# An audio tower on one core: the attention stage's chunk buffer, ScalarE's order in a step, and what is issued at the change of batch

## The reference, cut to what matters

```python
h = tokens(x)                                       # 8 batches x 376 tokens x 256
h = h + attn(layernorm(h))                          # 16 heads of 64: q,k,v; rope; causal softmax; @ Wo + bo
h = h + moe(layernorm(h))                           # top 2 of 4 experts: router, gates, w1, w3, w2
# attention, for each head:
sim = where(causal, q @ k.T * scale, -inf); attn = softmax(sim); out = attn @ v
# layernorm: (x - mean) / sqrt(var + 1e-5)
```

## Time and profile before

| what | us |
|---|---|
| median of 3 runs (lowest to highest) | 1735.87 (1735.42 to 1737.89) |
| the profiled execution, its own time | 1737.82 |
| its span, first to last instruction | 1736.0 |
| TensorE busy in the span | 1465.3 |
| ScalarE, VectorE, GpSimd busy | 958.4, 1183.6, 845.4 |

### The profile page before, as it was taken

The page is one execution under the profiler, slowest core; times in us unless marked ns, Lnnn a source line. Parts: engine busy times, 40 slices in busy tenths (PEclk is TensorE's granted clock), DMA queues, the critical chain, the costliest instruction groups (busy, mean ns, idle before and its releaser), DMA issues. The chain is left out here.

```text
span 1736.0 us, 30153 instructions
## 1 busy us (share of the span) xinstructions
PE 1465.3 (84%) x10725; PEld 1371.8 (79%) x10725; DVE 1183.6 (68%) x2590; ACT 958.4 (55%) x2093; POOL 845.4 (49%) x705
## 2 busy tenths in 40 slices
PE   5389999999989998998399999999998756789039
PEld 4279888888889897988399999999998746788039
DVE  7548676767677777775245666666577389459896
ACT  5547575757576757674244444445443344459552
POOL 4468575868576767762345555545544433000000
PEclk8679999999999999998599999999999868899569
DMA  7490202021111111010467666566565421003313
GB/s 244 145 316 19 73 19 80 31 80 32 59 34 56 52 58 52 4 35 4 154 223 210 182 202 206 180 188 211 177 196 149 89 86 38 10 2 133 118 46 112
DMA packets 91309, 186.94 MB, mean 108 GB/s; under 512 B 8568, under 2 KB 64184, under 8 KB 90904
## 3 DMA queue, kind: packets, MB, share of 16 engines
q1 hardware_dynamic: 80648, 171.19, 29.0%
q0 software_dynamic: 10512, 13.83, 4.7%
HBM read 139.01 MB, written 59.35 MB: 114 GB/s over the span
## 5 line engine op out<-in xcount | busy, mean ns | idle before, releaser
L1647 POOL TENSOR_TENSOR expert_w<-expert_raw,expert_w 128x768 fp32r<-128x768 f32 x95 | 181.9, 1915 | 241.9 <-ACT expert_w L1471 241.9
L1429 PE MATMUL psum<-slots_high,expert_w 128*128 128x384 f32 x1216 | 289.9, 339 | 6.4 <-DVE expert_act L1613 5.1
L879 ACT ACTIVATE expert_raw<-psum,neg_max 120x376 f32<-120x376 f32 (+2 forms) x384 | 176.8, 486 | 106.0 <-DVE neg_max L1083 103.8
L1429 PEld LDWEIGHTS psum<-slots_high,expert_w 128*128 128x128 f32 x1216 | 211.6, 190 | 10.0 <-issue 8.3
L1509 ACT ACTIVATE expert_act_high<-expert_act 128x384 fp32r<-128x384 f32 x152 | 79.8, 525 | 181.0 <-DVE expert_act L1613 181.0
L1106 DVE TENSOR_TENSOR pt_low<-psum,pt_high 128x752 fp32r<-128x752 f32 x128 | 120.5, 942 | 81.2 <-ACT pt_high L888 80.8
L1440 PE MATMUL psum<-expert_w,expert_act_high 128*128 128x256 f32 x912 | 173.2, 286 | 3.1 <-ACT slot_out L1491 3.0
L1002 POOL TENSOR_TENSOR qk_low<-rotated,qk_high 128x376 fp32r<-128x376 f32 x128 | 127.0, 992 | 95.9 <-ACT qk_high L872 95.9
L1618 DVE TENSOR_TENSOR expert_act_low<-expert_act,expert_act_high 128x384 fp32r<-128x384 f32 x152 | 109.8, 722 | 79.7 <-ACT expert_act_high L1509 79.7
L1429 PE MATMUL psum<-slots_low,expert_w 128*128 128x384 f32 x608 | 155.7, 337 | 0.0
L1440 PEld LDWEIGHTS psum<-expert_w,expert_act_high 128*128 128x128 f32 x912 | 145.4, 189 | 5.6 <-ACT slot_out L1491 3.9
(11 more groups left out here) (303 smaller groups left out, 3982.6 us busy)
## 6 DMA issues: line engine op xcount, KB each, us to landing
expert_w<-experts_split SPq DMA_DIRECT2D x57, 768.0 KB, 4.3
expert_raw<-in_experts SPq DMA_DIRECT2D x107, 384.0 KB, 5.2
x_slots<-in_c_slots SPq DMA_DIRECT2D x4, 3168.0 KB, 27.6
slot_rows<-x_slots SPq DMA_DIRECT2D x19, 396.0 KB, 5.3
up_spill<-held SPq DMA_DIRECT2D x5, 1128.0 KB, 5.0
held<-up_spill SPq DMA_DIRECT2D x5, 1128.0 KB, 6.1
experts_split<-pt_high SPq DMA_DIRECT2D x12, 384.0 KB, 2.4
experts_split<-pt_low SPq DMA_DIRECT2D x12, 384.0 KB, 3.2
```

The lines of the kernel that those rows point to most:

```text
L879: last = act.activation(probs[0:ni, h % 2, at:at + P * it + ni], score_bank(h % 2, it), ACT.Exp, bias=neg_max[0:ni, h % 2, it:it + 1], acc ...
L1429: last = pe.matmul(psum[:, 2 * k + g % 2, 0:TILE_SLOTS], w[hw][:, f, at:at + P], xt[hx][:, i % 2, c, :], start=(n == c == 0), stop=(n == 2 ...
L1647: pool.tensor_tensor(w[1][:, g % RING, :], raw[:, r % RAW, :], w[0][:, g % RING, :].bitcast(F32), ALU.subtract).then_inc(w_low, 1)
```

## The change

- `whole` gets a tile of its own. The load of the first chunk of the coming change is issued a batch earlier, behind the last store of this one (for the first: behind SP's work of batch 0), and waits for POOL's `parts_low` only, not for the rotations.
- To make room, `mask_f`, `ident_f` and `before_f` (read only in the stage before) lie in `shared`'s columns of the probabilities, and the four small tables of `tile_table` in `resid`.
- `begin(b)` on ACT: `deviation(b-1)` is issued ahead of the value copies of the second tile, behind the splits. A one-column exponential into `exp_warm` is issued ahead of those of the third tile.
- `step` on ACT: `spread_inverses(b, c)` and `scale_rows(b-1, (c,))` are issued behind `raw_copy` of step `c`, ahead of the first exponential, in place of the end of the step (the first `spread_inverses` leaves the prologue). The wait for `parts_low` goes from step 0; that for `parts_stored` stays.
- `step` on DVE: `swap_pairs(ahead + 1)` is issued ahead of `inverses(c + 1)`.

```diff
@@ attention
-        whole = shared[:, 0:CHUNK_COLS]
+        whole = sb("whole_w", [P, CHUNK_COLS])
+        warm = sb("exp_warm", [P, 1])
@@ block.sync
                 def load_whole(j):
                     e, k = SPLIT_JOBS[j]
+                    if j:
+                        sp.wait_ge(parts_low, j)
-                    sp.dma_start(whole, a["experts"][e, KEPT_SPLIT[k], :, :]).then_inc(whole_in, 16)
+                    sp.dma_start(whole[:], a["experts"][e, KEPT_SPLIT[k], :, :]).then_inc(whole_in, 16)
...
                 for b in range(BATCH + 1):
+                    if b == 1:
+                        load_whole(0)
                     if b in SPLIT_BATCHES:
-                        sp.wait_ge(rot_made, 16 * b + 2 * LEAD + CR_ROT)
-                        load_whole(2 * b - 2)
                         store_parts(2 * b - 2)
                         load_whole(2 * b - 1)
                         store_parts(2 * b - 1)
+                        if 2 * b < len(SPLIT_JOBS):
+                            load_whole(2 * b)
@@ block.scalar begin(b)
                         if at == 1 and b in SPLIT_BATCHES:
                             split_part(2 * b - 2)
                             split_part(2 * b - 1)
+                        if b and at == 1:
+                            deviation(b - 1)
+                        if b and at == 2:
+                            act.activation(warm[:], consts[:, EPS_LN:EPS_LN + 1], ACT.Exp)
                         for half in range(2):
...
-                        if b and at == 1:
-                            deviation(b - 1)
@@ block.scalar step(b, c, more)
                     if c == 0 and b in SPLIT_BATCHES:
-                        act.wait_ge(parts_low, 2 * b)
                         act.wait_ge(parts_stored, 64 * b)
                     turned_high(b, 2 * c)
                     if c:
                         out_high(b, c - 1)
                     if projects:
                         raw_copy(b, ahead)
+                    spread_inverses(b, c)
+                    if b and c < T:
+                        scale_rows(b - 1, (c,))
...
-                    if more or c + 1 < PAIRS:
-                        spread_inverses(b, c + 1)
-                    if b and c < T:
-                        scale_rows(b - 1, (c,))
@@ block.vector step(b, c, more)
+                    if projects:
+                        swap_pairs(b, ahead + 1)
                     if more or c + 1 < PAIRS:
                         inverses(b, c + 1)
-                    if projects:
-                        swap_pairs(b, ahead + 1)
                     scale_out(b, c)
```

More of the change, by code:

```diff
@@ L69 @@
 STEPS_TO_NORM = 17
-TABLES = ("x_parts", "rope_sin", "attn_bo", "x_rows", "mask", "ident_b", "mask_f", "ident_f", "router_w", "router_bias",
-          "moe_consts", "row_ids", "before_f", "before", "ones_b", "slot_base")
+TABLES = ("x_parts", "rope_sin", "attn_bo", "x_rows", "mask", "ident_b", "router_w", "router_bias",
+          "moe_consts", "row_ids", "before", "ones_b", "slot_base")
 def attention_tables(nc, ctx):
@@ L81, in attention_tables @@
         sb("x_rows", [P, 2, TILES, ROW]), sb("mask", [P, 2, P], BF16), sb("ident_b", [P, 2, P], BF16),
-        sb("mask_f", [P, 2, P]), sb("ident_f", [P, 2, P]), sb("router_w", [P, 2, EXPERTS]),
+        sb("router_w", [P, 2, EXPERTS]),
         sb("router_bias", [P, EXPERTS]), sb("moe_consts", [P, MOE_COLS]), sb("row_ids", [P, ALL_TILES]),
-        sb("before_f", [P, P]), sb("before", [P, P], BF16), sb("ones_b", [P, P], BF16), sb("slot_base", [P, EXPERTS]))}
+        sb("before", [P, P], BF16), sb("ones_b", [P, P], BF16), sb("slot_base", [P, EXPERTS]))}
 def tokens_in(nc, psum, a, consts, ident, vec, decay, first, weights, h0_rows, x_dram, tables, cos, made):
@@ L445, in attention @@
         T = TILES
-        x, sin, bo, rows, mask, ident_b, _, _, w, bias, cm, ids, _, before, ones_b, base = (tables[n] for n in TABLES)
+        x, sin, bo, rows, mask, ident_b, w, bias, cm, ids, before, ones_b, base = (tables[n] for n in TABLES)
         wq, wk, wv = ([w.rearrange("p (c n) -> p c n", c=2) for w in weights[n]] for n in range(3))
@@ L490, in attention @@
         ends = sb("tile_ends", [P, EXPERTS])
[L491 to L494, removed]
+        past = resid[:, 0, 0:EXPERT_TILES * EXPERTS].rearrange("p (t e) -> p t e", e=EXPERTS)
+        place = resid[:, 1, 0:2 * EXPERT_TILES].rearrange("p (k t) -> p k t", k=2)
+        owner = resid[:, 1, 2 * EXPERT_TILES:3 * EXPERT_TILES]
+        start_of = resid[:, 1, 3 * EXPERT_TILES:4 * EXPERT_TILES]
         slots_cleared = sem("slots_cleared")
@@ L927, in split_part @@
                     act.wait_ge(parts_stored, 32 * j)
-                    act.activation(parts[0], whole, ACT.Copy).then_inc(parts_high, 1)
+                    act.activation(parts[0], whole[:], ACT.Copy).then_inc(parts_high, 1)
                 def begin(b):
@@ L981, in _ @@
                 exps(0, 1, TILE_ORDER)
-                spread_inverses(0, 0)
                 qk_split(0, 2 * LEAD - 2)
@@ L1006, in split_part @@
                     pool.wait_ge(parts_high, j + 1)
-                    pool.tensor_tensor(parts[1], whole, parts[0].bitcast(F32), ALU.subtract).then_inc(parts_low, 1)
+                    pool.tensor_tensor(parts[1], whole[:], parts[0].bitcast(F32), ALU.subtract).then_inc(parts_low, 1)
                 def scatter(b, pieces):
@@ L2368, in audio_tower @@
             tables = attention_tables(nc, attn)
+            mask_f, ident_f, before_f = (shared[:, 5 * TOK + at:5 * TOK + at + n] for at, n in ((0, 2 * P), (2 * P, 2 * P), (4 * P, P)))
+            tables |= {"mask_f": mask_f.rearrange("p (k n) -> p k n", k=2), "before_f": before_f,
+                       "ident_f": ident_f.rearrange("p (k n) -> p k n", k=2)}
             tokens_in(nc, psum, a, consts, ident, vec, decay, first, weights, h0_rows, x_dram, tables,
```

## The result

The changed kernel takes 1692.07 us, the median of 4 runs (1690.77 to 1693.29), against 1736.48 (1735.42 to 1737.89, 4 runs) for the kernel before on the same chip. The ratio is 0.9744, with a 95% interval from 0.9727 to 0.9761: faster by 44 us. The forecast was 1699. The profiled execution took 1693.09, its span is 1691.3, so the two profiled executions differ by 44.7 us.

A forecast was written before the change was run, and what follows sets the result against it. A ring through DVE and ACT was taken to pace attention steps, with chunk stores and a table load delaying step 0. 23.9 + 15.2 + 1.7 + 1.5 = 42.3, less about 4, left 38: 1699 us, range 1691 to 1706.

The forecast's parts named there:

- The mechanism: In attention, a loop of waits through DVE and ACT paces steps; chunk loads, stores and a table load delay step 0.
- The seven steps 0: First step behind each change of batch: 8.15 us each, together 80.94 down to 57.05, gaining 23.9 us.
- steps 1 to 6: Attention steps of batches 1 to 6: 50.85 against 53.39 us per batch, gaining 15.2 us in all.
- One sign: In step 0 behind a change, `pt_high` would be released by TensorE, not by a DMA; starting 1.6 us earlier.
- 4 us off for ties: Four chains in the new order within 0.1 us: 0.07 us off for each of 60 steps, leaving 38 of 42.3.
- the ring: Attention steps: DVE and ACT waiting on each other in a loop, 8.77 us, shrinking to 7.87, below TensorE's 8.1.
- GpSimd as the next bound of the scatter steps: In attention steps with a scatter, POOL's 7.82 us busy and 0.37 of small gaps would limit at about 8.2.
- changes alone: Rival: only the changes of batch gain, steps stay at 8.3 or more; gain 24 to 28, 1709 to 1712; chance 0.2.
- The margin of step 0: Behind a change, the second chunk's stores would land about 0.9 us before TensorE ends the turn that `pt_high` needs.
- steps alone pay: Rival: second chunk's load and stores keep `pt_high` late at six changes, copies late too; gain 26, 1711; chance 0.1.
- Swap blocks the reciprocal: Rival: DVE's swap waits for the second projection, costing 1.1 us in each of 61 steps; 1779 us; chance 0.04.
- It doesn't do what it says: Rival: table reload stays ahead of the first exponential, ACT's new work fills its gap; within 3 of 1736; chance 0.05.

The follow-up runs named there:

- the runs with the orders apart: From the changed kernel, VectorE's step order put back: 1704.46 us; in another run, ScalarE's step order put back instead: 1707.62 us.
- the first two experiments: The changed kernel with both step reorderings put back, 1713.68 us; the kernel before with only those two reorderings made, 1714.55 us.

## Why the prediction was right, and where its sizes were off

**The mechanism held in each step.** The rows that show it are the unhindered split at 355.38, `deviation`'s table load at 364.39, the second at 367.20 ahead of the one-column exponential, and the exponential at 373.27 with none; in the step, the swap ahead of the reciprocal. The seven steps 0 gained 23.5 (predicted 23.9), steps 1 to 6 15.6 (15.2), batch 7 1.8 (1.7), batch 0 1.3 (1.5), step 7 -0.9 (0): 41.3 where 42.3 were summed. The warm exponential and the deviation cost nothing at the copies, as said; with either of them elsewhere each change lost about 1 us. One sign failed in part: `pt_high` of step 0 was to be released by TensorE, and in the changes to batches 1, 2 and 6 it was still released by the stores.

**The term that was mis-sized: 4 us off for ties.** It rested on no row. Plain steps came at 8.17 in place of 8.1 (0.07, which is the tie's size), but those with a scatter came at 8.15 to 8.18 in place of 8.25, so the two errors cancel and the discount had nothing to stand for: the steps gained 18.7 of the 18.4 summed.

**A stretch taken at 0 that gave 3.2 us, though not through the change's parts.** From the last first projection to the expert matmuls the kernel before took 81.3 us, the changed one 78.1, but the kernel with the buffer and early load alone, in which these steps are as before, took 77.8 (768.52 to 846.30). All eleven other kernels took 77.2 to 79.6 here, whatever their parts; it is the profiled execution of the kernel before that is long. Windows 12 to 18 us behind the last first projection, before and then after:

```profile
793.70:799.70 6.00, 5.17 (x26) 5.02 (x26) 4.43 (x11) 4.28 (x16) 0.59 (x2) 0.63 0.01 3
```

```profile
752.04:758.04 6.00, 4.78 (x48) 4.48 (x47) 4.77 (x12) 4.30 (x16) 1.53 (x2) 1.00 0.01 3
```

The granted clock (third number from the end) was down to a mean of 0.63 of full there, and 1.00 after: 26 matmuls against 48 in six microseconds. What decides it in this thin end of the stage, where all kernels dip at some place, is open. So of 44.7 us some 41 are the change's parts, against 42.3 summed and 38 forecast; the 3.2 are luck as far as is known.

**A claim that was wrong without harm.** "With the ring out of the way a plain step can't go below about 8.1 us" read TensorE's busy 8.13 as its content. The content is 7.87 to 7.88, shown by step 0 of batch 3 and by the plain steps with the first maximum moved; the rest of the 8.13 went without any work being taken out. GpSimd as the next bound of the scatter steps at 8.2 was wrong too; what came next was a third ring: turn, `pt_high`, `pt_low`, `o_low`, swap, maximum, exponential, `pt_high`, `pt_low`, mix. Moving one maximum in it brought 10.8 us.

**Slips in the working.** In the earlier trace rows step 1 has one instruction more not only on ScalarE (21 against 20) but also on GpSimd (9 against 8), so these rows alone didn't show that ScalarE's was the one that mattered; the runs with the orders apart did. The price of "changes alone" doesn't follow from its terms: 23.9 and 0.5 for each of 18 steps are 32.9, not 24 to 28. And 1699.8 less 1.95 is 1697.9, not 1699. None of them decides whether the forecast holds.

**The margin of step 0 was thin, not 0.9 us.** The second load was put at 3.76 us, as in the change to batch 2; the other five changes of the same kernel show 3.7 to 4.9. After, it took 4.1 us in the change to batch 3 (issue 359.43, split 363.53), and 5.7 in the change to batch 6 (issue 611.75); ScalarE and TensorE there, then ScalarE's first `pt_high` of batch 1's step 0:

```profile
617.44 0.84 ACT L933 ACTIVATE pt_high<-whole_w 128x768 fp32r<-128x768 f32 x1 [8.90 <-DMA whole_w<-in_experts]
```

```profile
624.25 0.50 PE L673 MATMUL psum<-mask,ident_b 64*128 64x128 bf16 x12 [0.92 <-DVE v_low L1238]
```

```profile
201.74 0.80 ACT L893 ACTIVATE pt_high<-psum 128x752 fp32r<-128x752 f32 x1 [1.15 <-DMA experts_split<-pt_low]
```

Step 0 of batch 6 took 9.01, for a late second load, and that of batch 1 8.81, for `pt_high` waiting 1.15 us for the stores. In batch 2 that wait was 0.42, and the step took 8.10. So what "steps alone pay" names came true in part in three changes of six, for 2.3 us above 7.87 in all where it was priced at 12. In all nine kernels with the early load the second load of batch 6 took 5.5 to 5.7 us, in the three without 3.9 to 4.7; so it comes with the early load, but which transfer it meets there stays open.

**The rivals.** "Changes alone" and "steps alone" fell by the first two experiments as forecasts of this kernel's time. "Swap blocks the reciprocal" needed the second projection 2.8 us later than in the kernel before; the swap starts at 300.02 without a wait. "It doesn't do what it says" fell by the rows of the change.

## What to carry to other kernels

Where several engines pass work in a ring, an order is worth as much as work: after each cut look for the next ring, by the smallest idle time that recurs ahead of the first instruction of a step, and ask what it can hold. A bound of "the engine is busy 8.1 of 8.4" is no floor; take the content from a step in which the engine waits for nobody. And take no discount that no row carries.

## What the runs showed of the hardware

- A table load doesn't always wait with the instruction it serves. Ahead of the square root of the deviation it ran at 364.39 in the kernel after, while the moments ended at 365.27. Ahead of the first exponential, in the kernel without the warm one, it ran only at 374.79, behind the wait for `neg_max`. What decides which was not tested.
- An addition of 0.41 us took 2.06 beside GpSimd's low part, and that took up to 2.26 in place of 1.85. The Trainium skill (SBUF — State Buffer, "Who interferes with whom") says that a VectorE instruction with two SBUF inputs contends with a GpSimd instruction that reads SBUF, and that the order of issue decides who blocks. The trace agrees; VectorE and GpSimd in the change to batch 3:

```profile
356.13 0.70 DVE L1129 TENSOR_TENSOR resid<-resid,attn_bo 128x512 f32<-128x512 f32 x1
356.75 2.06 DVE L1131 TENSOR_TENSOR resid<-resid,attn_bo 120x256 f32<-120x256 f32 x1
```

```profile
356.30 2.23 POOL L1011 TENSOR_TENSOR pt_low<-whole_w,pt_high 128x768 fp32r<-128x768 f32 x1
```

  The low part starts inside the first addition and takes 0.38 us longer than its 1.85; the second addition starts inside the low part and ends 0.28 us behind it (358.81 against 358.53). These times fit each waiting for the one that was there first.
- From 150 to 740 us the granted clock fell from 2.4 to 1.2 GHz in one kernel only, that with the late load, in four places: after waits of TensorE of 1.99 to 2.75 us at the mask, not after those of 1.87 and 1.56. It cost 1.4 us each time beyond the wait.
